# A seven-pass graph network: the units of a node pass run as two groups, one a part behind the other

## The reference, cut to what matters

```python
edge_index = jnp.stack([src, dst])
h = jnp.maximum(_layernorm(x, axis=-1), 0.0)
x = x + _L0_gnn_ref(h, edge_attr_8, node_vec1, ...)      # message, segment sum, bilinear update, silu
h = jnp.maximum(_layernorm(x, axis=-1), 0.0)
x = x + _L1_gnn_ref(h, edge_index, edge_attr_8, ...)     # edge-conditioned convolution
h = jnp.maximum(_layernorm(x, axis=-1), 0.0)
x = x + _L2_gnn_ref(h, edge_attr_8, src, dst, ...)       # encoder, two message passing rounds, decoder
h = jnp.maximum(_layernorm(x, axis=-1), 0.0)
x = x + _L3_gnn_ref(h, edge_index, edge_weight, ...)     # two GCN convolutions
```

## Time and profile before

| | us |
|---|---|
| median of three timed runs | 17686.4 |
| the profiled execution's own time | 17701.2 |
| its span from the first to the last instruction | 17699.5 |
| TensorE busy, share of the span | 13912.2, 79% |
| VectorE busy | 13068.0, 74% |
| ScalarE busy | 7125.3, 40% |
| GpSimd busy | 4621.6, 26% |
| mean granted TensorE clock | 0.819 |

### The profile page before, as it was taken

How to read it: one execution, slowest core, us unless ns; L and a number is a source line. 1 busy time by engine, 2 the same in 40 slices (tenths; PEclk the granted TensorE clock), 3 DMA queues, 4 the chain that set the end, 5 groups by cost and what they waited for, 6 DMA issues and landing times. The chain is left out here.

```text
span 17699.5 us, 504368 instructions
## 1 busy us (share of the span) xinstructions
PE 13912.2 (79%) x180289; PEld 12124.8 (69%) x180600; DVE 13068.0 (74%) x30392; ACT 7125.3 (40%) x15316; POOL 4621.6 (26%) x4403
## 2 busy tenths in 40 slices
PE   1677776777767997799999999996799999856565
PEld 0566666666654997588888888885577777646565
DVE  2888888888866997566656656665677777779899
ACT  0454454544542332344444444443344444411111
POOL 0677777777760110011111111110000000001111
PEclk9666666666656998899999999997899999967676
DMA  1122222222222553344444444442444444437566
GB/s 60 54 57 59 57 60 58 57 59 57 60 54 76 157 156 99 96 116 123 117 118 119 118 119 119 121 118 75 131 151 154 154 152 150 132 92 210 167 210 177
DMA packets 1347419, 1956.45 MB, mean 111 GB/s; under 512 B 705453, under 2 KB 923253, under 8 KB 1306317
## 3 DMA queue, kind: packets, MB, share of 16 engines
q1 hardware_dynamic: 1046674, 1621.50, 29.5%
q0 software_dynamic: 209664, 186.01, 7.5%
q10 hardware_dynamic: 90300, 137.10, 2.1%
HBM read 1443.57 MB, written 501.97 MB: 110 GB/s over the span
## 5 line engine op out<-in xcount | busy, mean ns | idle before, releaser
L828 POOL DMA_INDIRECT records<-e_sort_rec,e_sort_index x3224 | 3295.8, 1022 | 1347.4 <-issue 920.3
L2411 PEld LDWEIGHTS e_s_ps_h<-e_s_pick,e_s_parts 128*64 128x64 bf16 x61776 | 1965.7, 113 | 298.7 <-issue 137.0
L2411 PE MATMUL e_s_ps_h<-e_s_pick,e_s_parts 128*64 128x128 bf16 x61776 | 2028.9, 223 | 108.7 <-issue 108.7
L1165 PE MATMUL e_sort_acc<-e_sort_thirds,e_sort_hot 128*128 128x48 f32 x6864 | 1488.8, 414 | 301.4 <-DVE e_sort_hot L992 301.4
L1165 PEld LDWEIGHTS e_sort_acc<-e_sort_thirds,e_sort_hot 128*128 128x128 f32 x6864 | 1472.1, 332 | 332.1 <-DVE e_sort_hot L992 332.1
L2530 POOL DMA_DIRECT2D states<-e_s_second_t x520 | 480.3, 924 | 4176.9 <-ACT e_s_second_t L2259 4108.3
L2006 DVE TENSOR_SCALAR e_s_pick<-e_s_rows,lane_below 128x1024 bf16<-128x1024 bf16 (+1 forms) x3120 | 1179.1, 434 | 372.2 <-PE e_s_ps_h L2411 350.7
L2046 DVE TENSOR_TENSOR e_s_unit<-e_s_ps_o,lane_out 128x512 f32<-128x512 f32 (+1 forms) x520 | 324.9, 625 | 1421.0 <-PE e_s_ps_o L2369 1420.7
L2521 POOL DMA_INDIRECT e_s_spill<-send,e_s_lists x208 | 218.3, 1049 | 3633.1 <-PE e_s_ps_h L2433 2741.9
L1082 ACT ACTIVATE e_sort_away<-iota,e_sort_slots 128x128 f32<-128x128 f32 x3640 | 1107.5, 388 | 10.1
L2444 PE MATMUL e_s_ps_o<-w_eblk,e_s_act 128*128 128x128 f32 x7488 | 1015.1, 276 | 98.2 <-DVE e_s_unit L2055 81.6
(11 more groups left out here) (558 smaller groups left out, 31254.5 us busy)
## 6 DMA issues: line engine op xcount, KB each, us to landing
e_s_rows<-rows_d SPq DMA_DIRECT2D x312, 1088.0 KB, 5.3
e_s_hot<-hots_d SPq DMA_DIRECT2D x520, 560.0 KB, 3.9
e_s_to_rows<-rows_d SPq DMA_DIRECT2D x208, 608.0 KB, 5.9
e_s_rows<-rows_d SPq DMA_DIRECT2D x208, 544.0 KB, 4.4
e_s_rows<-rows_d SPq DMA_DIRECT2D x208, 512.0 KB, 5.2
e_s_to_rows<-rows_d SPq DMA_DIRECT2D x208, 512.0 KB, 6.2
states<-e_s_first_t ACTq DMA_DIRECT2D x416, 256.0 KB, 2.1
states<-e_s_second_t POOLq DMA_DIRECT2D x416, 256.0 KB, 4.2
```

The costliest lines, as they stand in the source:

```text
L828: pool.indirect_dma_start(records, bass.IndirectOffsetOnAxis(ap=index[x][:, t:t + 1], axis=0), rec[x][:, t, :], None,).then_inc(written[x] ...
L1165: mm = pe.matmul(acc[sum_bank(c)][:, sum_at(c)], hot[:, c, :], thirds[:, c, :, :].rearrange("p h f -> p (h f)"), start=False, stop=last an ...
L2411: mm = pe.matmul(halves[half][:, j * LANES:(j + 1) * LANES], parts[:, SPAN * c + h, r, :], pick[p][:, h, (c - c0) * LANES:(c - c0 + 1) * L ...
```

## The change

The five units of a turn are split into two groups: units 0, 1 and 2 (`LEADING`) and units 3 and 4 (`FOLLOWING`). The steps of a pass are cut into parts, at the steps named in a new argument `opens`. Every engine now goes through rounds: in a round it issues one part of the leading group and then one part of the following group, which is `lag` parts behind, across the borders of turns. At the start of a turn VectorE waits only for the units of its own group. The instructions themselves, their semaphores and steps, the loads and the stores are as before. `node_pass`, the three loops that call the bodies, and one body as an example (all others are changed in the same way, `range(K)` to `now(step)`):

```diff
+    LEADING, FOLLOWING = range(0, (K + 1) // 2), range((K + 1) // 2, K)
-    def node_pass(name, loads, tables, stores, steps, dve_body, act_body, pe_body, bufs, bigs, turns):
+    def node_pass(name, loads, tables, stores, steps, dve_body, act_body, pe_body, bufs, bigs, turns, opens, lag):
+        part_of, part = {}, 0
+        for step in steps:
+            part += step in opens
+            part_of[step] = part
+        n_parts = len(opens) + 1
+        def rounds():
+            for r in range(NODE_TURNS * n_parts + lag):
+                for units, late in ((LEADING, 0), (FOLLOWING, lag)):
+                    if 0 <= r - late < NODE_TURNS * n_parts:
+                        yield (units,) + divmod(r - late, n_parts)
+        def among(units, part):
+            def now(step):
+                return units if part_of[step] == part else ()
+            return now
...
-            for i in range(NODE_TURNS):
-                if i:
-                    for u in range(K):
+            for units, i, part in rounds():
+                if i and part == 0:
+                    for u in units:
                         dve.wait_ge(q[u].sem, q[u].end(i - 1))
-                dve_body(dve, q, ready, i, t=turns[i % 2])
+                dve_body(dve, q, ready, among(units, part), i, t=turns[i % 2])
...
-    def node_newton(dve, q, ready, p, i, value, out_, t):
+    def node_newton(dve, q, ready, now, p, i, value, out_, t):
...
-        for u in range(K):
+        for u in now(names[1]):
             dve.wait_ge(*ready(u, names[1], i))
```

More of the change, by code:

```diff
@@ L3062, in _ @@
             def _(act):
-                for i in range(NODE_TURNS):
-                    act_body(act, q, ready, i, t=turns[i % 2])
+                for units, i, part in rounds():
+                    act_body(act, q, ready, among(units, part), i, t=turns[i % 2])
         if pe_body is not None:
@@ L3068, in _ @@
             def _(pe):
-                for i in range(NODE_TURNS):
-                    pe_body(pe, q, ready, i, t=turns[i % 2])
+                for units, i, part in rounds():
+                    pe_body(pe, q, ready, among(units, part), i, t=turns[i % 2])
         for u in range(K):
@@ L3133, in ln_relu @@
             dve.tensor_tensor(squares[u], centered[u], centered[u], ALU.mult).then_inc(q[u].sem, 1)
-        node_norm_stats(dve, q, ready, p, i, squares, F, v)
-        for u in range(K):
+        node_norm_stats(dve, q, ready, now, p, i, squares, F, v)
+        for u in now(f"{p}_norm"):
             dve.wait_ge(*ready(u, f"{p}_norm", i))
@@ L3146, in ln_affine @@
                               ALU.mult).then_inc(q[u].sem, 1)
-        for u in range(K):
+        for u in now(f"{p}_gain"):
             dve.wait_ge(*ready(u, f"{p}_gain", i))
             dve.tensor_tensor(o[u], o[u], gb[k][:, 0, :].unsqueeze(1).broadcast_to([P, C, D]), ALU.mult).then_inc(q[u].sem, 1)
-        for u in range(K):
+        for u in now(f"{p}_bias"):
             dve.wait_ge(*ready(u, f"{p}_bias", i))
@@ L3232, in n1_dve @@
                                   bc3(flat(t["al"][u][:, 0:2, :]), [P, 2 * F, F]), ALU.mult).then_inc(q[u].sem, 1)
-            for u in range(K):
+            for u in now("upd_prod1"):
                 dve.wait_ge(*ready(u, "upd_prod1", i))
@@ L3236, in n1_dve @@
                                   bc3(flat(t["al"][u][:, 2:4, :]), [P, 2 * F, F]), ALU.mult).then_inc(q[u].sem, 1)
-            for u in range(K):
+            for u in now("upd_sum"):
                 dve.wait_ge(*ready(u, "upd_sum", i))
@@ L3240, in n1_dve @@
                                   op=ALU.add).then_inc(q[u].sem, 1)
-            for u in range(K):
+            for u in now("x_upd"):
                 dve.wait_ge(*ready(u, "x_upd", i))
@@ L3297, in n1_pe @@
                 pe.matmul(ps[u][0:TW, 0:P], flat(t["h"][u]), ident[:, :], start=True, stop=True).then_inc(q[u].sem, 1)
-            for u in range(K):
+            for u in now("y"):
                 pe.wait_ge(*ready(u, "y", i))
@@ L3349, in n2_dve @@
                                   ALU.add).then_inc(q[u].sem, 1)
-            for u in range(K):
+            for u in now("x_new"):
                 dve.wait_ge(*ready(u, "x_new", i))
@@ L3392, in n2_pe @@
                 last.then_inc(q[u].sem, 1)
-            for u in range(K):
+            for u in now("out"):
                 pe.wait_ge(*ready(u, "out", i))
                 by_node(pe, ps[u], t["a"][u], W["nenc1"][:, :], D, row["nenc1"]).then_inc(q[u].sem, 1)
-            send_recv_pe(pe, q, ready, i, t, ps, 0, "n")
+            send_recv_pe(pe, q, ready, now, i, t, ps, 0, "n")
         node_pass("n2", [("x", x1_d)], (agg1, 1),
@@ L3479, in _gnn, with n4_dve @@
     with st:
-        def n4_dve(dve, q, ready, i, t, ps=ps):
-            node_update_dve(dve, q, ready, i, t, ps, 1)
-            for u in range(K):
+        def n4_dve(dve, q, ready, now, i, t, ps=ps):
+            node_update_dve(dve, q, ready, now, i, t, ps, 1)
+            for u in now("dec_bias"):
                 dve.wait_ge(*ready(u, "dec_bias", i))
```

266 lines of the change are left out of this document (133 added, 133 removed).

## The result

The changed kernel takes 17,596.97 us (median of five runs, 17,584.12 to 17,602.52), before it was 17,686.4 in five runs beside them: a ratio of 0.9947 with a 95% interval of 0.9933 to 0.9962, 89 us or 0.5% less. 17,573 was forecast, and the measured time lies inside the range and in the likeliest case's own range. Its profiled execution has a span of 17,582.5 at a granted clock of 0.822 (before 17,699.5 at 0.819).

A forecast was written before the change was run, and what follows sets the result against it. Neither bytes nor engine throughput but the chain inside a turn bounds n1 to n5; loads and stores pace n0 and n6. Terms -88, -27, -39, +20, -7, 0, +28 sum to -113: 17,588 profiled, 17,573 median; range 17,515 to 17,660.

The forecast's parts named there:

- the likeliest case: The forecast itself, 17,573, with its own range 17,538 to 17,613; chance .72.
- n2: Node pass: the groups' alternate parts use different engines, turn 37.9, 195.5 in place of 283.5, -88 us.
- n1: Node pass: both groups' parts want the same engines, nothing overlaps and fillings are paid twice, +20 us.
- The three terms of the sum: In n1, hand-over fillings paid twice: +1.9 in parts 0 and 1, +3.2 in part 2, 1.8 back in part 3.
- n6: Node pass: without store 0 no load 2, so load, work and store of one turn follow each other, +28 us.
- n3: Node pass: the following group's first part starts behind the leading group's second; turn 45.6 in place of 52.0, -27 us.
- F part 0: In n3 and n4, the following group's first part, 2 units, taken as 2/5 of 30.4: 12.2 us a turn.
- rival four: Loads bind n3 and n4; if twice as long beside stores, +36 and +26, together 17,635; chance .08.
- n4: Node pass: first two parts the same code as n3's, turn 48.0 in place of 56.4, -39 us.
- n0 and n5: Node passes: n0's load-work-store chain, 34.4 for two turns, saves 2.8, -7 us; n5 bound by loads and stores, 0.
- The clock: TensorE's granted clocks, 0.50 in n1 and 0.57, 0.70, 0.65 in n2 to n4, left as they were.
- The slower rival: Groups only take turns everywhere, one filling of about 1 us per part and turn, +103, 17,789; chance .07.

## Why the prediction was right, point by point

- **n2**: right in mechanism and size. Its turn came out 0.8 shorter than worked out and its last three stores, now closer together, landed 2.8 later (the last one's issue to the next stage 11.0 in place of 8.2); the two nearly cancel.
- **n1**: right, +25.5 for +20. Each round's parts want the same engine, and the leading group's next part stands behind the following group's first. The rows of n1 show F's wait becoming L's: its sum and first matmuls stand in front of L's `h_turned` for 7.8 us. That the order is the cause two runs bear out: as one group again n1 returned to 316, and with other cuts, groups of two and three and the same lag it fell to 257. The three terms of the sum (+1.9, +3.2 and -1.8 a turn) come from no row; the turn grew by 5.1 for the 4 forecast.
- **n6**: right, +26.3 for +28, by the chain named. Without the lag it is gone.
- **n3**: the sign is right, the size half (-12.9 for -27). The mis-sized term is F part 0, taken as 2/5 of 30.4 or 12.2: it took 13.6 on average, 7 us over five turns, with TensorE at 0.60 to 0.63 in four of them, where part 0 of five units had 0.69 in the first two turns of the kernel before, each from the part's first matmul on. The sum "leaves all clocks as they were"; inside this part that didn't hold. Second, rival four: "46.1, against 45.6" was taken as no cost, and a sign that the prediction had named as showing it wrong, VectorE's first sum in n3 waiting for a DMA, came true; it cost 4.8 us. Third, the last stores landed 4.3 later, since three of them now follow within 6 us (13.0 in place of 8.7). Some smaller terms came out 2 us shorter together; that makes up the 14 us missed.
- **n4**: mechanism right, size off (-26.9 for -39). The mis-sized term is F part 0 again, 13.6 on average for 12.2, 7 of the 12 us. And `dec_bias` stood 1.4 behind the other group's norm, which the sum had put beside it. Per turn 50.4 in place of 48.0.
- **n0 and n5**: within 4 us, but not by the bounds that were named. Their first sums, in n0 before and after, in n5 before and after:

```profile
323.35 0.72 DVE L3124 TENSOR_REDUCE n_v<-n_x_odd 125x4 f32<-125x64 f32 x5 [11.54 <-ACT n_y L3202]
337.12 0.47 DVE L3146 TENSOR_REDUCE n_v<-n_x 125x4 f32<-125x64 f32 x3 [12.83 <-DMA n_x<-in_x]
16694.65 3.62 DVE L3539 TENSOR_REDUCE n_s<-n_tab_odd 125x64 f32<-125x384 f32 x5 [0.23 <-DVE n_o L3543]
16560.45 2.21 DVE L3561 TENSOR_REDUCE n_s<-n_tab 125x64 f32<-125x384 f32 x3 [6.12 <-DMA n_tab<-agg]
```

  Before, both passes waited for the last product of the turn before, not for a load; loads bind them only after the change. n0's two turns were 37.1 and not the 34.4 of its chain, and fell to 32.6. n5's 0 is luck: its turn without a lag is 10.9 in place of 12.0, and under the lag it waits for loads, 6.1 to 6.6 us in three turns, which takes the gain away.
- **The clock**: that all clocks stay as they are held for n1 and, over the windows, roughly for n3 and n4; n2's rose from 0.57 to 0.63, and inside the parts of n3 and n4 it moved both ways, as told above. Without the lag it rose further, to 0.84 in n3.
- **The slower rival** (the groups take turns everywhere) failed by the condition it was given: in n2 the following group's sum began while TensorE was busy with the other group. With no cuts and no lag it was true in part: n4 and n1 lost 42 and 10 us, while n2 and n3 still gained 35 and 25.

What the prediction didn't ask is whether the lag itself helps. It worked the lag's queue order out faithfully, and found the 12.2 us of n3's following part in front of the leading group's last part, without noting that with no lag they could lie beside the leading norm. The lag cost some 200 of the 288 us that the same groups and cuts give without it (n3 76, n4 54, n1 42, n6 27, n5 6).

## What to carry to other kernels

Two groups overlap only where the part that is queued behind finds another engine free, so write the rounds down as "what stands behind what on each engine", and try a lag of 0 first: a part placed behind a *later* part of the other group can hold that group's next step too. A lag isn't wrong in every case: with n1's new cuts a lag of 2 was worth 20 us. Where a load waits for the end of *all* units, a lag lengthens the time from load to release and can turn two turns in flight into one. A part of few units can take longer than its share of the units (13.6 for 12.2 here, with a lower clock in it), so give it a range; and price loads that come out within 1% of the turn as binding.

## What the runs showed of the hardware that was not expected

- An issue on SyncE's queue right behind three stores took 4.76 and 5.55 us, the same two 0.26 and 1.61 when the stores had landed. An earlier issue was worth less here than the wait that it replaced.
- In n1 TensorE was granted 0.50 of its clock, 1.2 GHz, in all four kernels whose window of n1 is shown, busy for 63 to 82% of the window, while n3 had 0.84 with 77%. What decides it stays open; no run here tells it apart.
- A pass of the same order and the same matmuls took up to 5.6 us more in another execution, with TensorE busy longer at a lower granted clock: n3 281.9 and 287.5 us (busy 166.2 and 171.4, clock 0.70 and 0.68), n2 206.2 and 210.9 (163.1 and 169.9, 0.61 and 0.58). Differences of that size in these passes say nothing by themselves.
- A stage that no kernel touched varied by 44 us over the profiled executions, half of the change's whole effect; among four kernels on one chip it was 12 us.
